# Slice attention on one core: TensorE takes the logits before the temperature sums, and the first transposes of the exponentials before the output product

## The reference

```python
# t: tokens (32 images, 256 positions, 64 channels); 8 heads of 16; 16 slices g per head
x_proj = (x @ W_x.T + b_x).reshape(B, N, H, D).transpose(0, 2, 1, 3)
adaptive_temp = BASE_TEMP + jnp.clip(x_proj @ W_temp.T + b_temp, -0.4, 0.4)
slice_logits = x_proj @ W_slice.T + b_slice - log_neg_log_eps
slice_weights = jax.nn.softmax(slice_logits / adaptive_temp, axis=2)   # over the positions
slice_norm = slice_weights.sum(axis=2)
eidetic = jnp.einsum('bhnc,bhng->bhgc', x_proj, slice_weights)
eidetic = eidetic / (slice_norm + 1e-05)[..., None]
out_x = jnp.einsum('bhgc,bhng->bhnc', eidetic, slice_weights)
return out_x.transpose(0, 2, 1, 3).reshape(B, N, H * D) @ W_out.T + b_out
```

## Time and profile before

| What | Value |
|---|---|
| Time of the profiled execution | 1367.41 us |
| Its span, first to last instruction | 1365.6 us |
| Median of three executions | 1367.01 us |
| PE matmul busy over the span | 1045.2 us (77%) |
| DVE busy | 848.6 us (62%) |
| ACT busy | 519.7 us (38%) |
| Mean granted clock of TensorE | 0.772 |
| First project of slice attention | 338.14 us |
| Last output product of slice attention begins | 465.87 us |
| First matmul of the layer normalisation behind it | 471.08 us |

### The profile page before, as it was taken

How to read it: one execution, slowest core, us unless ns; L and a number is a source line. 1 busy time by engine, 2 the same in 40 slices (tenths; PEclk the granted TensorE clock), 3 DMA queues, 4 the chain that set the end, 5 groups by cost and what they waited for, 6 DMA issues and landing times. The chain is left out here.

```text
span 1365.6 us, 27455 instructions
## 1 busy us (share of the span) xinstructions
PE 1045.2 (77%) x9710; PEld 611.4 (45%) x9710; DVE 848.6 (62%) x2482; ACT 519.7 (38%) x1338; POOL 264.8 (19%) x375
## 2 busy tenths in 40 slices
PE   6778786767988756666666666666973899999996
PEld 2356652253666535454454545453542333333332
DVE  6586845745556365555555555554346688888885
ACT  3443442453443323232323232223641545554452
POOL 3303012300000000000000000000100255555555
PEclk9898997868999865555555555557985999999998
DMA  6000002000000000000000000000000775555650
GB/s 226 1 1 1 1 2 78 0 1 1 1 0 0 1 1 0 0 0 0 0 0 0 0 0 0 0 0 1 0 1 8 146 149 130 123 123 121 131 117 23
DMA packets 23059, 47.41 MB, mean 35 GB/s; under 512 B 1616, under 2 KB 5840, under 8 KB 22608
## 3 DMA queue, kind: packets, MB, share of 16 engines
q1 hardware_dynamic: 22992, 46.51, 14.7%
HBM read 43.88 MB, written 2.62 MB: 34 GB/s over the span
## 5 line engine op out<-in xcount | busy, mean ns | idle before, releaser
L1613 PE MATMUL wide<-ls_h,ls_v 128*128 128x16 f16 x2304 | 104.1, 176 | 144.4 <-DVE ls_h L1712 141.2
L2115 ACT ACTIVATE ex_gated<-wide,unscale 128x1024 f32<-128x1024 f32 x128 | 142.1, 1113 | 138.8 <-PE wide L2081 138.7
L2131 DVE TENSOR_TENSOR ex_hid<-wide,ex_gated 128x1024 f32<-128x1024 f32 x128 | 156.0, 1223 | 44.5 <-ACT ex_gated L2115 40.0
L1613 PEld LDWEIGHTS wide<-ls_h,ls_v 128*128 128x128 bf16 x2304 | 81.0, 105 | 213.4 <-DVE ls_h L1712 213.4
L2057 POOL TENSOR_TENSOR ex_acc<-ex_part,ex_acc 128x512 f32<-128x512 f32 x120 | 152.3, 1270 | 94.9 <-DVE ex_part L2147 80.7
L1702 DVE TENSOR_TENSOR_SCAN ls_cells<-ls_terms 128x48 f32<-128x48 f32 x256 | 73.6, 288 | 124.1 <-ACT ls_terms L1637 124.1
L1637 ACT ACTIVATE ls_terms<-wide 128x32 f32<-128x32 f32 x256 | 54.4, 213 | 229.6 <-PE wide L1618 229.6
L2093 PE MATMUL wide<-ex_hid,w 128*64 128x512 f32 x512 | 116.7, 598 | 0.0
L2081 PE MATMUL wide<-xh,wh 64*128 64x512 f16 x512 | 98.8, 382 | 4.6 <-PEq L81 3.2
L2081 PE MATMUL wide<-xh,wl 64*128 64x512 f16 x512 | 98.0, 379 | 0.0
L2081 PE MATMUL wide<-xl,wh 64*128 64x512 f16 x512 | 97.8, 378 | 0.0
(11 more groups left out here) (364 smaller groups left out, 1925.4 us busy)
## 6 DMA issues: line engine op xcount, KB each, us to landing
ex_d<-route SPq DMA_DIRECT2D x64, 512.0 KB, 7.9
par_attn<-in_attn SPq DMA_DIRECT2D x1, 2704.0 KB, 13.3
par_rest<-in_rest SPq DMA_DIRECT2D x1, 2539.0 KB, 18.6
L_xin<-in_x SPq DMA_DIRECT2D x8, 256.0 KB, 5.6
w<-in_w SPq DMA_DIRECT2D x1, 2048.0 KB, 7.9
out<-ex_acc SPq DMA_DIRECT2D x16, 128.0 KB, 4.6
w<-in_w SPq DMA_DIRECT2D x1, 512.0 KB, 8.9
route<-ro_dt SPq DMA_DIRECT2D x8, 64.0 KB, 1.7
```

The costliest lines, as they stand in the source:

```text
L1613: pe.matmul(ig[:, g, :] if g < 2 else o, vp[part][:, g, :], h1[:], start=False, stop=False, skip_group_check=True)
L2115: act.activation(gated[:, n % 2, :], pair_of_up(n // GS, 2 * (n % GS))[:], ACT.Silu, scale=m.unscale[:, 0:1]).then_inc(s["gated_ready"], 1)
L2131: dve.tensor_tensor(hid[:, n % (2 * GS), :], pair_of_up(n // GS, 2 * (n % GS) + 1)[:], gated[:, n % 2, :], ALU.mult).then_inc(s["hid_ready ...
```

## The change

PE's program order in a step changes in two places; no instruction is added or removed, and no other engine's code changes. logits(0) goes ahead of the temperatures. turn(0) goes from its place behind logits(1) to one ahead of the output product. The new order of a full step is: by_token(0), logits(0), temperatures, turn(0), output product, by_token(1), logits(1), turn(1), GT product, and the rest as before. In step 0, which has no output product, turn(0) stands ahead of by_token(1) and logits(1).

```diff
                 if first:
                     by_token(0)
+                    logits(0)
                     temperatures()
-                    logits(0)
+                if second:
+                    turn(0)
                 if third:
                     pe.wait_ge(s["bm_ready"], t + 1)
                     for b in range(2):
@@ -1343,7 +1345,6 @@
                     by_token(1)
                     logits(1)
                 if second:
-                    turn(0)
                     turn(1)
                     pe.wait_ge(s["gtm_ready"], t + 1)
                     pe.wait_ge(s["xpt_ready"], 2 * t + 3)
```

## The result

The changed kernel takes 1349.49 us (median of seven, 1347.94 to 1352.93) against 1367.01 us; the ratio is 0.9881, with a 95% interval of 0.9863 to 0.9899. It is faster, as forecast, and by more than forecast: the median lies 0.5 us under the range's lower end of 1350.0, while the ratio times 1367.01 gives 1350.7.

What follows compares the result with a forecast made beforehand. PE's order from output product to GT, then the chain through bm, bounds a step. Order 8.2 + 0.9 + 1.8 = 10.9 us, clock +2.9, sum 13.8 off 1367.41; named 1353.2 us, range 1350.0 to 1358.2.

Steps and rivals of the forecast that it cites:

- What bounds a step: Loop step of 14.65 us: PE's own order from output product to GT product, then a 4.31 us chain to bm.
- The swap at nothing: Loop: logits(0) ahead of the temperatures gains nothing by itself, since bm sets the end; it makes room.
- turn(0) hidden: Loop: turn(0) starts at 395.33 and ends by 395.93, 0.95 us before the output product, covered by the chain to bm.
- 8.2 us in six steps: Six steps with output product and `first` part: GT 3.63 us behind the product, gaining 1.36 each; bounds 0.6 and 1.41.
- what is late next is the copy of the second tokens: Loop: the copy ends 3.56 us behind the output product's start, so GT could start at 3.61, level with PE's order at 3.62.
- Step 0, 0.9 us: Step 0: turn(0) waits for exponentials, PE pauses some 1.3 us, yet GT starts at 357.16 instead of 358.08.
- Rival C: Step 0: the clock falls in a 1.3 us PE pause; 1355.1 to 1361.1 us, for one time 1358; chance 0.08.
- Step 7 order, 1.8 us: Step 7 at half clock: GT comes at about 457.94 instead of 459.78, with turn(0) hidden before bm.
- The clock at the end, +2.9, bounds 0 and 5.1: Steps 7 and 8: clock back about when GT begins; GT gains 1.35 us, the last output product 1.56.
- case A: Order gains, and the clock at the stage's end comes back early; 1351.5 to 1355.5 us; chance 0.52.
- D: Step 7: no half clock at all, since turn(0) splits the 3.03 us pause; 1351 us; chance 0.12.
- F: Slower: the clock falls inside the loop before the output product; some 1396 us if throughout; chance 0.05, half a smaller fall.

Runs made afterwards that it cites:

- experiment 1: Kernel before with only logits(0) moved ahead of the temperatures, turn(0) left in place: 1367.54 us, ratio 1.0005.
- experiment 2: Kernel before with only turn(0) moved ahead of the output product, temperatures still ahead of logits(0): 1350.12 us, ratio 0.9879.
- experiments 9 and 10: Whole change plus logits(1) ahead of the output product, 1346.59 us; then also DVE's second token copy ahead of the output's addition, 1347.00 us.
- experiment 5: Whole change, but in step 0 turn(0) stands behind logits(1) as before: one time, 1349.45 us.
- experiment 3: Whole change, but in step 7 turn(0) stands behind the output product as before: 1354.35 us, ratio 0.9912.
- run 6: Whole change, but turn(0) stands first in the step, ahead of by_token(0): 1358.99 us, ratio 0.9944.
- experiment 4: Kernel before, with turn(0) ahead of the output product in step 7 only: 1360.47 us, ratio 0.9954.
- run 7: Whole change plus project(0) ahead of turn(0) and the output product: 1345.68 us, ratio 0.9855.

## Why the prediction was right, and where it was off

- **What bounds a step** was right: PE's order from product to GT, and the chain through bm from there. The pause on ACT's copy went, the one on bm stayed (0.79 to 0.80).
- **The swap at nothing**: right, by experiment 1. That it "makes room" was needless by experiment 2.
- **turn(0) hidden**: right. It was done by 390.81, 0.80 before the product.
- **8.2 us in six steps**: measured 8.62, or 1.44 a step, a little above the 1.41 that was named as the upper bound. The step that failed is "what is late next is the copy of the second tokens". It is not waited for at all (experiments 9 and 10); GT starts when turn(1) has gone through, 0.44 behind it, where I had carried over the 0.49 of a turn that came out of a wait. Two limits that lay 0.01 apart hid the error: that the number was nearly right was in this part luck, and it would have been 0.86 a step wrong for the next change.
- **Step 0, 0.9 us**: 1.02 from the first project to product(1), and 0.94 when undone alone. Rival C (the clock falls there) did not come. Its premise was wrong as well: the pause is not turn(0)'s, PE waits as long there for DVE's token copy without it (experiment 5).
- **Step 7 order, 1.8 us**: right at half clock; at full clock it is 1.41 (experiment 3).
- **The clock at the end, +2.9, bounds 0 and 5.1**: mis-sized; 5.1 to 5.5 came. I gave case A 0.52 and D 0.12, and D is what all three traces of this program show. Runs 5, 6, 9 and 10, which have the same order in step 7 and other times ahead of it, come close to A: one fall in step 7, back at full clock by the GT product or inside it. D's reason, that turn(0) splits the pause, is not what decided it: in experiment 3 the pause was whole and the clock stood through step 7 all the same.
- The three terms off, 0.4, 0.1 and 2.2, are the 2.75 by which the stage beat 13.8. The remaining 1.75 us between the profiled executions (1.35 ahead of the stage, 0.4 behind it) lie in code that is the same.
- **The chances** have a slip: A to E add up to 0.95 and not 0.94, and half of F leaves 0.025 for slower, not 0.04. It changes nothing in the forecast.

Whether the clock falls in step 7 depends on two things, and the runs separate them. In all 14 traces the clock rose to 1.00 between 8.37 and 8.57 us behind the stage's first project, so times can be counted from that rise. With product(7) 106.8 us behind it, the clock fell with the old order of step 7 (the kernel before twice, and experiment 1) and not with the new one (experiment 4): there turn(0)'s place decides. With product(7) at 97.2 to 97.4 us, it fell in step 7 with neither (the changed kernel three times and experiment 2; experiment 3 with the old order), and at 98.3 us it fell with the new order (experiment 5): there the moment decides. At other moments it stayed up once with the new order (93.1 us, run 7) and fell three times (92.1 and 92.2 us, runs 9 and 10; 105.0 us, run 6). So the full clock of the changed kernel is a matter of order and of timing, and each of the three repeats had the same timing. What the moment is to be measured against, and so which moments are safe, stays open.

## What to carry to other kernels

In an engine with a hand-written order, look for the wait that another engine's chain sets in any case, and move work under it from the part of the step in which this engine is itself the bound; a swap of two groups that both lie under that wait gains nothing. What is moved must have its inputs ready by then: the same transposes three groups earlier lost 0.86 us a step. Before a copy is named the next limit, check which tile and which buffer it writes: level times in a trace are no dependence, and a run that takes the work between them away shows it. When part of a gain comes from the clock, price order and clock apart, and don't add the gains of two changes that both touch the same fall of the clock.

## What the runs showed of the hardware

- The clock is worth a large part of such a change: 5.5 of the 16.55 us in the stage came from work in steps 7 and 8 (both output products, the turns, the GT product) that ran at 2.4 instead of 1.2 GHz, and the pattern repeated in all three traces of the changed kernel and both of the kernel before.
- Transposes held the clock up: at equal timing it fell 2.0 us into the pause of 3.03 us in the kernel before, and not with four float32 transposes in that pause (experiment 4).
- The moment counts: at equal order, step 7 at 98.3 instead of 97.3 us behind the clock's rise had some 3 us at half clock (experiment 5).
- Code that no kernel here changed took different times ahead of the stage: its first project began at 331.6 us (run 10) to 340.1 us (run 6) over 14 traces, with some 74 us at half clock in the first and 97 us in the second up to there (mean granted clock 0.89 and 0.86). Single times of one kernel scatter accordingly (1356.95 to 1369.97 us for the kernel before), so the gains of a microsecond were read from the stage in the traces, where the order part repeats to 0.05 us. Runs 7, 9 and 10 have lower medians than the changed kernel by 2.5 to 3.8 us, but their intervals overlap with its own; that they beat it rests on the step of 12.4 to 12.5 against 13.23.
